# A graph layer's projection phase: half of the rows of h turned by a transposing transfer, statistics eight pairs ahead

## The reference

```python
h = jnp.maximum(_layernorm(x, axis=-1), 0.0)
mask = (adj > 0).astype(x.dtype)
deg = jnp.sum(mask, axis=1, keepdims=True)
agg = mask @ h / jnp.maximum(deg, 1.0)
self_f = h @ W_self + b_self
nb_f = agg @ W_nb + b_nb
out = jnp.concatenate([self_f, nb_f], axis=-1) @ W_comb + b_comb
return x + relu(out)
```

## Time and profile before

| | |
|---|---|
| runs | 1001.7, 1001.33, 1002.5 us; median 1001.7 |
| profiled execution | 1001.76 us, of which the span is 1000.0 us |
| TensorE, VectorE, ScalarE, GpSimd busy | 99%, 67%, 59%, 3% of the span |
| projection phase, TensorE | from 14.5 us to 110.5 us |
| 64 row tiles | from 110.5 us, about 13.84 us each |

### The profile page before, as it was taken

One profiled execution on the slowest core, in us unless ns is written; L12 is line 12 of the kernel. 1 busy time (PEld: TensorE's weight loads), 2 busy tenths in 40 slices (PEclk: granted clock), 3 DMA queues, 4 the chain that ended last, 5 costly groups with the idle time before them and its releaser, 6 DMA issues.

```text
span 1000.0 us, 14269 instructions
## 1 busy us (share of the span) xinstructions
PE 989.9 (99%) x4696; PEld 460.5 (46%) x4696; DVE 673.9 (67%) x1163; ACT 585.0 (59%) x675; POOL 30.5 (3%) x73
## 2 busy tenths in 40 slices
PE   7999999999999999999999999999999999999998
PEld 4555444444444444444444444444444444444443
DVE  6886677986776666766667666676666766667711
ACT  5888886775655556655556555565555655556500
POOL 2332000000000000000000000000000000000000
PEclk9999999999999999999999999999999999999999
DMA  9621399999888898888988888888888888888600
GB/s 344 251 85 43 140 421 371 416 420 377 320 316 321 312 341 317 319 322 312 342 312 322 322 313 336 318 322 322 312 328 328 323 315 321 321 326 326 218 16 10
DMA packets 58994, 295.04 MB, mean 295 GB/s; under 512 B 6624, under 2 KB 24160, under 8 KB 26208
## 3 DMA queue, kind: packets, MB, share of 16 engines
q1 hardware_dynamic: 58976, 294.81, 78.6%
HBM read 286.39 MB, written 8.39 MB: 295 GB/s over the span
## 4 chain that ended last, share of the span: by engine, by line
PE 98%; DMA 1%; DVE 0%; SPq 0%; issue 0%
PE pair_ps L360 89%; PE pair_ps L351 8%; PE turn_ps L333 1%; DMA self_f<-in_x_dram 1%; PE pair_ps L381 0%; DVE x_again L439 0%; SPq L195 0%; SPq L193 0%; DVE z L505 0%; DVE fold L502 0%; DVE x_again L442 0%; DVE part L485 0%; DVE part L482 0%; DVE x_again L488 0%; SPq L177 0%
## 5 line engine op out<-in xcount | busy, mean ns | idle before, releaser
L360 PE MATMUL pair_ps<-z,mask_t 128*128 128x512 f16 x4096 | 885.8, 379 | 0.0
L290 ACT ACTIVATE mask<-mask 128x2048 uint8<-128x2048 uint8 x256 | 488.0, 1908 | 341.4 <-DVE mask_t L430 341.4
L360 PEld LDWEIGHTS pair_ps<-z,mask_t 128*128 128x128 fp8e4 x4096 | 396.2, 98 | 475.7
L430 DVE STREAM_TRANSPOSE mask_t<-mask 128x512 uint32<-128x512 uint32 x256 | 181.7, 710 | 219.8 <-PE pair_ps L360 214.3
L424 DVE TENSOR_SCALAR mask<-stage 128x2048 uint8<-128x2048 int32 x256 | 308.1, 1203 | 6.0 <-DMA stage<-in_adj_dram 5.9
L351 PE MATMUL pair_ps<-mask_t 128*128 128x512 f16 x384 | 87.8, 379 | 0.0
L351 PEld LDWEIGHTS pair_ps<-mask_t 128*128 128x128 f16 x384 | 37.6, 98 | 38.6
L290 ACT ACTIVATION_READ_ACCUMULATOR mask<-mask 128x1 f32 x256 | 48.1, 188 | 0.0
L482 DVE SCALAR_TENSOR_TENSOR part<-pair_ps,rdeg,self_f 128x256 f32<-128x256 f32 x64 | 31.0, 484 | 15.7 <-DVE rdeg L477 11.9
L269 ACT ACTIVATE self_f<-self_f,x_again 128x256 f32<-128x256 f32 x64 | 35.0, 605 | 8.7 <-POOL x_again L260 8.7
L447 DVE SCALAR_TENSOR_TENSOR mask_t<-turn_ps,mask_t 128x512 f16<-128x512 f32 x32 | 21.8, 681 | 19.3 <-ACT mask_t L276 19.3
(11 more groups left out here) (31 smaller groups left out, 93.0 us busy)
## 6 DMA issues: line engine op xcount, KB each, us to landing
stage<-in_adj_dram SPq DMA_DIRECT2D x256, 1024.0 KB, 5.9
self_f<-in_x_dram SPq DMA_DIRECT2D x16, 512.0 KB, 15.4
x_again<-in_x_dram SPq DMA_DIRECT2D x64, 128.0 KB, 5.3
out_dram<-x_again SPq DMA_DIRECT2D x64, 128.0 KB, 5.1
z<-in_L_gnn_W_comb_dram SPq DMA_DIRECT2D x2, 256.0 KB, 4.8
z<-in_L_gnn_W_self_dram SPq DMA_DIRECT2D x1, 256.0 KB, 3.6
z<-in_L_gnn_W_nb_dram SPq DMA_DIRECT2D x1, 256.0 KB, 4.5
z<-in_L_gnn_b_comb_dram SPq DMA_DIRECT2D x1, 128.0 KB, 6.4
```

The source lines that it names most:

```text
L290: act.activation(mask[:, a, :], mask[:, a, :], ACT.Copy, accum_out=deg_part[:, n, a:a + 1]).then_inc(counted, 1)
L360: mm = pe.matmul(acc[n], bytes_of[:, :, s], z16[:, SUB * e + s, :], start=(e == 0 and s == 0), stop=(e == CHUNKS - 1 and s == SUB - 1))
L430: dve.transpose(mask_t[:, n, :, a, :], src).then_inc(transposed, 1)
```

## The change

Of each pair only the first 128 rows go through TensorE, ScalarE and VectorE as before, with half as many elements (`turn`, `high_of_h`, `low_of_h`). The second 128 rows take a new way: GpSimd casts them to fp16 (`cast`), VectorE subtracts to get the rest (`rest_of_h`), and SyncE issues a transposing transfer of both halves, 128 x 512 fp16, from SBUF to SBUF (`move`), into a ring of four places (PLACES). The source ring has three (HALVED), so `cast(j)` waits until `move(j-3)` has landed. `project(j)` waits for `move(j)` too. `norm` runs four pairs ahead instead of three, the statistics eight instead of six. The loads of x from the sixth chunk on, and of the first mask quarters, are issued between the moves, and the loads for the second row tile after the last move.

```diff
+PLACES = 4
+HALVED = 3
+STATS_AHEAD = {0: (6, 7), 1: (8, 9)}
+LOAD_STEPS = (1, 7, 13, 19)
...
+            def move(j):
+                at = j % PLACES
+                sp.wait_ge(h_rest, j + 1)
+                if j >= PLACES:
+                    sp.wait_ge(projected, j - PLACES + 1)
+                    sp.wait_ge(h_moved[at], (j // PLACES) * DONE)
+                sp.dma_start_transpose(h_t[:, at, 1, :, :, :].rearrange("p i h m -> p (i h) m"),
+                                       h16[:, j % HALVED, :, :].rearrange("p i d -> p (i d)")
+                                       ).then_inc(h_moved[at], DONE)
...
-            for e in range(2, 6):
+            for e in range(2, 5):
                 load_x(e)
-            for a in range(QUAD):
-                load_group(0, a)
-                load_x(6 + a)
-            for e in range(6 + QUAD, CHUNKS):
-                load_x(e)
+            for j in range(PAIRS):
+                e = j // 2 + 5
+                if j % 2 == 0 and e < CHUNKS:
+                    load_x(e)
+                if j in LOAD_STEPS:
+                    load_group(0, LOAD_STEPS.index(j))
+                move(j)
...
-            for e in range(CHUNKS):
+            def rstd_of(e):
                 pool.wait_ge(aggr_done, SUB * (e + 1))
...
+            def cast(j):
+                pool.wait_ge(normed, 2 * (j + 1))
+                if j >= HALVED:
+                    before = j - HALVED
+                    pool.wait_ge(h_moved[before % PLACES], (before // PLACES + 1) * DONE)
+                pool.tensor_copy(h16[:, j % HALVED, 0, :], self_f[:, 2 * j + 1, :]).then_inc(h_cast, 1)
+
+            rstd_of(0)
+            rstd_of(1)
+            for j in range(PAIRS):
+                cast(j)
+                if j in (0, 3, 4):
+                    rstd_of((2, 3, 4)[(0, 3, 4).index(j)])
+                if j >= 6 and j % 2 == 0 and j // 2 + 2 < CHUNKS:
+                    rstd_of(j // 2 + 2)
...
-                for t in range(2):
-                    for half in range(HALVES):
-                        at = (t * HALVES + half) * P
-                        mm = pe.transpose(turn_ps[j % 2][:, at:at + P], self_f[:, 2 * j + t, half * P:(half + 1) * P],
-                                          ident)
+                for half in range(HALVES):
+                    mm = pe.transpose(turn_ps[j % 2][:, half * P:(half + 1) * P],
+                                      self_f[:, 2 * j, half * P:(half + 1) * P], ident)
...
                 pe.wait_ge(h_low, j + 1)
+                pe.wait_ge(h_moved[j % PLACES], (j // PLACES + 1) * DONE)
...
+            def rest_of_h(j):
+                dve.wait_ge(h_cast, j + 1)
+                dve.scalar_tensor_tensor(h16[:, j % HALVED, 1, :], self_f[:, 2 * j + 1, :], 1.0,
+                                         h16[:, j % HALVED, 0, :], ALU.mult, ALU.subtract).then_inc(h_rest, 1)
...
             w_low(0)
+            rest_of_h(0)
             w_low(1)
             low_of_h(0)
             for p in range(4, 6):
                 stats_of(p)
+            rest_of_h(1)
+            rest_of_h(2)
             dve.wait_ge(c_product, 1)
...
                     low_of_h(j + 1)
+                if j + 3 < PAIRS:
+                    rest_of_h(j + 3)
                 if j >= 2:
                     low_of_z(j - 2)
-                if j + 6 < PAIRS:
-                    stats_of(j + 6)
+                for p in STATS_AHEAD.get(j, (j + 8,)):
+                    if p < PAIRS:
+                        stats_of(p)
```

More of the change, by code:

```diff
@@ L85, in graph_layer @@
         PAIR = 2 * 2 * HALVES * P
-        h_t = spare[:, 0:RING * PAIR].rearrange("p (n i t h m) -> p n i t h m", n=RING, i=2, t=2, h=HALVES)
-        w12 = spare[:, RING * PAIR:RING * PAIR + 4 * HALVES * D].rearrange("p (i h n) -> p i h n", i=2, h=HALVES)
+        W_AT = PLACES * PAIR
+        H_AT = W_AT + 4 * HALVES * D
+        h_t = spare[:, 0:W_AT].rearrange("p (n t i h m) -> p n t i h m", n=PLACES, t=2, i=2, h=HALVES)
+        w12 = spare[:, W_AT:H_AT].rearrange("p (i h n) -> p i h n", i=2, h=HALVES)
+        h16 = spare[:, H_AT:H_AT + HALVED * 2 * D].rearrange("p (n i d) -> p n i d", n=HALVED, i=2)
         late = z16[:, 3 * TILES // 4:, :].rearrange("p t n -> p (t n)").bitcast(F32)
@@ L150, in graph_layer @@
         h_low = sem("h_low")
+        h_cast = sem("h_cast")
+        h_rest = sem("h_rest")
+        h_moved = [sem(f"h_moved{n}") for n in range(PLACES)]
         projected = sem("projected")
@@ L273, in high_of_h @@
                 act.wait_ge(h_turned, j + 1)
-                if j >= RING:
-                    act.wait_ge(projected, j - RING + 1)
-                act.activation(h_t[:, j % RING, 0, :, :, :].rearrange("p t h m -> p (t h m)"), turn_ps[j % 2][:, :],
+                if j >= PLACES:
+                    act.wait_ge(projected, j - PLACES + 1)
+                act.activation(h_t[:, j % PLACES, 0, 0, :, :].rearrange("p h m -> p (h m)"), turn_ps[j % 2][:, 0:D],
                                ACT.Copy).then_inc(h_high, 1)
@@ L301, in _ @@
             norm(2)
+            norm(3)
             for j in range(PAIRS + 1):
@@ L305, in _ @@
                     high_of_h(j + 1)
-                if j + 3 < PAIRS:
-                    norm(j + 3)
+                if j + 4 < PAIRS:
+                    norm(j + 4)
                 if j >= 1:
@@ L350, in project @@
                     for at, (half, i, w) in enumerate(steps):
-                        mm = pe.matmul(pair_ps[j % RING][:, t, :], h_t[:, j % RING, i, t, half, :], w12[:, w, half, :],
+                        mm = pe.matmul(pair_ps[j % RING][:, t, :], h_t[:, j % PLACES, t, i, half, :], w12[:, w, half, :],
                                        start=(at == 0), stop=(at == len(steps) - 1))
@@ L444, in low_of_h @@
             def low_of_h(j):
-                flat = "p t h m -> p (t h m)"
+                flat = "p h m -> p (h m)"
                 dve.wait_ge(h_high, j + 1)
-                dve.scalar_tensor_tensor(h_t[:, j % RING, 1, :, :, :].rearrange(flat), turn_ps[j % 2][:, :], 1.0,
-                                         h_t[:, j % RING, 0, :, :, :].rearrange(flat), ALU.mult, ALU.subtract
+                dve.scalar_tensor_tensor(h_t[:, j % PLACES, 0, 1, :, :].rearrange(flat), turn_ps[j % 2][:, 0:D], 1.0,
+                                         h_t[:, j % PLACES, 0, 0, :, :].rearrange(flat), ALU.mult, ALU.subtract
                                          ).then_inc(h_low, 1)
+            def rest_of_h(j):
+                dve.wait_ge(h_cast, j + 1)
+                dve.scalar_tensor_tensor(h16[:, j % HALVED, 1, :], self_f[:, 2 * j + 1, :], 1.0,
+                                         h16[:, j % HALVED, 0, :], ALU.mult, ALU.subtract).then_inc(h_rest, 1)
             def low_of_z(j):
```

## The result

The changed kernel takes 1017.39 us in the median (1016.78 to 1018.16, 4 runs) against 1001.81 for the kernel before (1001.33 to 1002.5, 4 runs). The ratio is 1.0151, 95% interval 1.0139 to 1.0164: slower, by 15 us. The forecast was 1016, with 1009 to 1027 around it.

The account below looks back on a forecast made before the run. TensorE bounds the kernel, but the new order makes VectorE wait on GpSimd rounds; a 7.1 us late start, 68.5 of rounds and a 19.0 tail put row tiles 14.3 later: 1001.76 + 14.3 = 1016.1 us, range 1009 to 1027.

Parts of the forecast that it names:

- The circle: Projection phase: VectorE waits for a GpSimd scale-and-shift round it has just released; 6.50 us for two pairs, 3.25 a pair.
- K: Time from the start of VectorE's BN_AGGR through GpSimd's round and cast to the start of `rest_of_h`: 2.61 us.
- The mask within the round: Rounds with a mask quarter: VectorE's mask work lies inside the wait, so a mask costs 0.88 us, not 1.9.
- The start: First steps up to `low_of_z(2)` in step 4: project(5) freed at 37.2 us instead of 30.09, 7.1 us late.
- The sum: Whole projection phase: rounds plus a TensorE-bound tail of 19.0 us put the row tiles at 124.8, 14.3 us later.
- Ten rounds: Steps 4 to 24: ten circles of 6.50 us, four with a mask at 0.88 more, 68.5 us in all.
- VectorE's waits for GpSimd: Sign in the changed profile: about 13 waits ahead of `rest_of_h`, 2.1 us or 1.1 with a mask, 23 us in all.
- The moves: Transposing transfers in the projection phase: wanted 7.1 us after issue, so hidden and costed at nothing.
- The bounds from the rows: Landing times of the nearest transfers for a move: 3.6 us for 256 KB, idle queue; 5.3 for 128 KB between mask loads.
- only some 6 us would be left: Cover for a move's landing if VectorE were not slow and pairs ran at 2.81 us, instead of 7.1 us.
- The covered round: Rival: VectorE's work hides GpSimd's round, K 1.73 us or less; phase gains 6.5 us, 995.3 us; chance 5%.

Follow-up runs that it names:

- the second experiment: Changed kernel with `rest_of_h` moved behind the statistics in VectorE's step, GpSimd's order unchanged: 1001.49 us, ratio 0.999 to the kernel before.
- the fifth experiment: Changed kernel with the four mask quarters one step earlier, in steps 4, 10, 16 and 22: 1021.75 us, ratio 1.0195 to the kernel before.
- the first experiment: Changed kernel with GpSimd's scale-and-shift rounds moved behind the odd cast of a chunk instead of the even one: 999.45 us, ratio 0.9976 to the kernel before.
- last experiment: On top of the first experiment, two source places for the moves instead of three (`HALVED = 2`): 1001.92 us, ratio 0.9997 to the kernel before.

## Why the prediction was right

**The circle.** Forecast 6.50 us for two pairs and 7.38 with a mask; measured 6.56 (30.25 to 36.81, 50.85 to 57.41) and 7.45. Two errors of the terms cancel. K was taken as 2.61 and is 2.49 (34.32 to 36.81): the cast is 0.40 as taken, but it starts 0.06 before the instruction ahead ends, and VectorE follows its end by 0.03, not 0.09. And `rest_of_h` behind a wait takes 0.51 to the next start, not 0.33, while the others take 0.33 (39.17 to 39.50).

That 0.51 has its own reason in the rows. GpSimd's second cast runs until 37.12; VectorE's subtraction starts at 36.81, ends at 37.40 and lasts 0.59, where the one at 39.17, with GpSimd idle, lasts 0.42. The Trainium skill (SBUF — State Buffer, "SBUF: two separate sides") says that VectorE and GpSimd hold a shared pair of ports exclusively, a VectorE instruction with two SBUF inputs included when the GpSimd one reads SBUF, so that the later one waits for the whole of the earlier. The trace agrees in the main: 0.28 of the work lies behind 37.12. At 25.71 only one cast was in the way (25.29 to 25.69), and the subtraction took 0.43. In the second experiment, where three subtractions start 0.02 to 0.06 ahead of a cast (at 90.95, 93.72 and 96.53), they keep their 0.41 and it is the cast that takes 0.61 to 0.65 instead of 0.40.

```profile
90.95 0.41 DVE L493 SCALAR_TENSOR_TENSOR mask_t<-self_f,mask_t 128x256 f16<-128x256 f32 x1
90.97 0.65 POOL L291 CAST mask_t<-self_f 128x256 f16<-128x256 f32 x1 [1.15 <-ACT self_f L309]
```

I had left this out of the sum; it is worth some 0.18 a circle.

**The mask within the round.** Forecast +0.88, measured +0.89, and +1.87 outside it, by the fifth experiment.

**The start.** Forecast project(5) at 37.2, measured 38.25. Of the 1.0, 0.4 is that the first loads came later in this execution: `w_low(0)` starts at 12.98, before any new wait, where I had taken 12.46; in the nine profiled executions it starts anywhere from 11.88 to 13.55. Another 0.4 are the two subtractions at 19.48, which took 1.05 instead of 0.66, beside GpSimd's casts. The shorter K, four times, and the longer `rest_of_h`, twice, nearly cancel. The last 0.3 is a term that I took too small: from the start of `low_of_z(2)` to project(5) are 0.93 (37.32 to 38.25), and the sum has 0.60, the distance to VectorE's next instruction.

**The sum.** Ten rounds: 68.5 forecast, 69.16 measured (38.25 to 107.41). From there to the row tiles 19.0 and 19.0. Together 15.9 instead of 14.3. VectorE's waits for GpSimd: 23 us forecast, 23.9 measured, which is closer than it deserves. The 23 counts 13 rounds, but the prediction's own list of steps has 14 (one ahead of the loop, steps 1 and 2, and eleven from 4 to 24), 25 us at 2.1 and 1.1. The trace has these 14 at 1.94 each (2.25 the first) and 0.96 with a mask, and one small wait at 14.02. The forecast time does not use that count, only the spread of its range does.

**The moves.** Costed at nothing; the two waits laid to them are 0.8 us of TensorE (project(1), while VectorE was the later one soon after) and 2.3 of GpSimd. They landed in 2.4 to 5.0 us, 2.6 in the median. The bounds from the rows, 3.6 and 5.3, were too high for most of them. So was the 5.2 estimated from the figure of the Trainium skill (VectorE: DVE Perf Modes, "The three transpose paths") for one block, taken four times: for this transfer, SBUF to SBUF, the measured time decides. The sentence that at 2.81 a pair "only some 6 us would be left" was borne out: with the circle open and three places it sufficed, with two it did not quite.

**The covered round.** The rival on the other side asked for K below 1.73; K is 2.49, and it fell. The gain that it priced, 6.5 us of TensorE's work, is real, though: the first experiment shows 2.81 us a pair, and loses some 3 of the 6.5 again at the start, where the first two projects wait for their moves (project(1) at 20.98, before at 17.98).

## What to carry to other kernels

An engine's share of busy time, above all as an average over the span, does not say whether it is on the path. When a step is given to an idle engine, look at what stands directly ahead of it in that engine's list, and who releases that; if it is the engine that will wait for the step, the two take turns, and the time of the circle, not the work of either, sets the pace. Two cures with the same instructions worked: put the step ahead of the round on the idle engine, or put enough of the waiting engine's own work between release and wait. A mechanism of this kind can be priced before it is run, from starts in the trace of before and the order of the two lists.

## What the runs showed of the hardware

A transposing transfer of 128 x 512 fp16 from SBUF to SBUF landed 2.4 us after issue at the least. Directly behind a load of x (0.5 MB) it took 2.9 to 7.5 us, behind one of the mask (1 MB) 4.1 to 8.5, in the traces of the first, second and last experiment. SyncE needs 1.19 us to issue one, against 0.58 for a load of x and 0.33 for one of the mask in the median, so that 32 of them are 38 us of its time; TensorE still ran at 2.81 us a pair beside them in the first experiment. Moving such transfers forward into a queue that was still full gained little: 2.3 us earlier out gave no earlier landing for the first, and 3.5 gave 1.3 for the second.

TensorE's clock fell for a moment in some of the starts. In the changed kernel TensorE was busy for 0.59 of the 2 us from 20 to 22; project(1), from 22.64, then took 4.35 us instead of 2.75, and the granted clock was 0.50 from 24 to 26, the 1.2 GHz level. It cost nothing there, since project(3) waits for VectorE all the same (1.59 us at 31.70).

```profile
22.64 4.35 PE L391 MATMUL pair_ps<-mask_t 128*128 128x512 f16 x12 [0.82 <-DMA mask_t<-mask_t]
31.70 2.75 PE L391 MATMUL pair_ps<-mask_t 128*128 128x512 f16 x12 [1.59 <-DVE z L498]
```
